# A row-fetched third tree, Silu in place in PSUM and a new order of work in a one-core layer of binding attention and tree feed-forward

## The chip, the cores and the metric

The kernel runs on one core of one Trainium2 chip. The metric is the device time of one execution, in microseconds. TensorE (PE) multiplies matrices, VectorE (DVE), ScalarE (ACT) and GpSimd (POOL) do the rest, and SyncE (SP) issues DMAs.

## The reference

Input x has 2 x 4096 tokens of D = 512. The layer is attention by binding, then a feed-forward made of trees, each on a layer norm and with a residual:

```python
q = unit(ln(x) @ Wq.T + bq); k = unit(...); v = unit(...)   # unit: FFT / (|FFT| + 1e-8)
s = cumsum(ifft(fft(k) * fft(v)).real, axis=tokens)
x = x + ifft(fft(s) * conj(fft(q))).real
logits = ln(x) @ W_in.T + b_in        # 8 trees of 255 nodes, 127 of them inner
# from the root, seven times: go right where the node's logit is positive
# dmap is 1 on the eight nodes of the path, in each tree
x = x + (silu(logits) * dmap) @ W_out.T
```

## The kernel before

Tokens go in 32 blocks of T = 256 (J = 2 halves of 128). The Fourier transform is folded into the projection weights in the prologue, so a projection gives the spectrum. Every product of TensorE is made of three fp16 products (high x high, high x low, low x high), so each operand is split in a high part by ScalarE (`high`, `act_high`, `fold_high`) and a low part by VectorE (`low`, `act_low`, `fold_low`). Weights stay in SBUF.

One queue per engine is written out by hand, and each engine runs its queue in order; semaphores join them. Each engine's program is `first()` (the prologue), `step(0)`, a loop over steps 1 to 29, and steps 30 and 31 written out. In `step(i)` the feed-forward of block i runs beside the attention of block n = i + 1:

- TensorE: `project(n, Q)`, K, V (48 matmuls each: a real part into `bank_p[0]`, then an imaginary one into `bank_p[1]`), `logits(i, t, c)` of tree t and its column slice c into `bank_l[t % 4]`, `counts(i, t)`, which adds the count of steps off the path, `down(i, j)` back to D, and the inverse transforms of block n (`transform_back`). Dense trees have two slices of 128 columns.
- Trees in `GATHERED` (0 and 1) have one dense slice, their inner nodes. For their last node on the path ScalarE's `leaf` marks it, one-column products give its number (`leaf_rows_of`, `leaf_row_copy`), POOL fetches its row of weights by an indirect DMA (`fetch`), VectorE multiplies (`leaf_dots`), ScalarE applies Silu (`leaf_silu`), and VectorE adds it (`leaf_add`).
- ScalarE: `evac_re` and `evac_im` of each projection, `square`, `root`, `high`, Silu of each tree into one of `HELD` = 3 buffers `acts` in SBUF, `act_high`. `logits` of tree t + 4 reuses a bank once Silu has read it.
- POOL: sums of squares, `add_eps`, `q_unit`, `bind` (four products k x v), the fetches, `unbind` (four products s x q, one after another) and its sums.
- VectorE: `residual`, statistics, low halves, reciprocals, `decide` (the comparison that feeds `counts`), `act_low`, the running sum, the small Nyquist operations (one frequency that is kept apart), leaf work and `result`.
- SP: the transposes of xn2 into `x2t` (for the logits) and of xn1 into `xt` (for the next projections), two DMAs each, and all loads and stores.

The prologue loads the projection weights, folds them (`fold_tile`), finds a scale for each of five groups of weights (Q, K, V, G_IN, G_OUT; ScalarE's `..._rows` sum absolute values, VectorE's `peak_of`, `peak_row` and `scale_group` follow), splits them, and does block 0's attention.

## Time and profile before

| | |
|---|---|
| median of 3 runs | 1975.06 us (1973.09 to 1975.19) |
| span of the profiled execution | 1972.4 us |
| outside its span | not listed; the median is 2.7 us above the span, the fastest run 0.7 us |
| TensorE busy | 1883.7 us, 96% of the span |
| VectorE busy | 1579.8 us, 80% |
| ScalarE busy | 1118.8 us, 57% |
| POOL busy | 917.0 us, 46% |

The page gives one execution of the program. Busy times of matmuls include their pipelined ends, so a busy TensorE isn't one at its peak. The prologue and step 0 last to 154.7 us, steps 1 to 30 to 1913.5.

### The profile page before, as it was taken

Reading aid. Unit: us, or ns where it says so; the run is one execution under the profiler, and the core shown is the slowest. Engines: PE = TensorE matmul, PEld = TensorE weight load, DVE = VectorE, ACT = ScalarE, POOL = GpSimd, SP = SyncE. Lnnn points to the kernel's source line nnn. Section 1 sums busy time; section 2 is a strip of 40 time slices with the busy share of each in tenths; the row PEclk is TensorE's granted clock in tenths of the full one; section 3 lists DMA queues with packets and bytes.
Section 4 is the critical chain, followed back from the end, with each engine's and each line's share of the span. In section 5 each row is a group of like instructions: output and inputs, shape, how many; then the busy total and the mean of one; then the engine's idle time right before and its main releaser. Section 6 shows DMA issues by size and latency. Waiting matters only on the chain.

```text
span 1972.4 us, 40210 instructions
## 1 busy us (share of the span) xinstructions
PE 1883.7 (96%) x14680; PEld 1410.5 (72%) x14680; DVE 1579.8 (80%) x2874; ACT 1118.8 (57%) x2151; POOL 917.0 (46%) x736
## 2 busy tenths in 40 slices
PE   8599999999999999999999999999999999999978
PEld 6468777777777777877777877777777777786755
DVE  4887888887888888788888788888788888878783
ACT  5566555566555556555556655556655555655543
POOL 1254444555444555444555444455544455534450
PEclk9799999999999999999999999999999999999998
DMA  8032133222223222223222213222222322222212
GB/s 278 11 86 87 54 96 95 65 85 85 64 85 96 75 80 80 82 67 96 83 77 85 85 53 96 94 66 85 85 64 85 96 75 79 81 71 79 86 54 65
DMA packets 181784, 163.18 MB, mean 83 GB/s; under 512 B 140160, under 2 KB 140800, under 8 KB 181760
## 3 DMA queue, kind: packets, MB, share of 16 engines
q1 hardware_dynamic: 163328, 95.48, 16.2%
q0 software_dynamic: 18432, 67.38, 10.2%
q8 instruction: 15, 0.25, 0.0%
q14 instruction: 9, 0.07, 0.0%
HBM read 95.72 MB, written 16.78 MB: 57 GB/s over the span
## 4 chain that ended last, share of the span: by engine, by line
PE 74%; DVE 10%; ACT 6%; issue 3%; DMA 0%; ACTq 0%; SPq 0%; DVEq 0%
PE bank_l L531 26%; PE bank_p L481 24%; PE bank_l L591 17%; DVE arena L1220 9%; ACT arena L796 3%; ACT arena L705 2%; PE bank_i L481 2%; PE bank_l L541 2%; ACT arena L806 1%; PE bank_i L552 1%; PE bank_i L562 0%; PE bank_i L559 0%; PE bank_i L560 0%; PE bank_i L561 0%; DVE sp_z L1178 0%
## 5 line engine op out<-in xcount | busy, mean ns | idle before, releaser
L591 PE MATMUL bank_l<-wout_mem,arena 128*128 128x512 f16 x2688 | 606.7, 379 | 38.6 <-DVE arena L1220 38.6
L531 PE MATMUL bank_l<-arena,win_mem 128*128 128x256 f16 x5376 | 626.0, 273 | 14.0 <-DMA arena<-xn_pair 14.0
L531 PEld LDWEIGHTS bank_l<-arena,win_mem 128*128 128x128 f16 x5376 | 527.5, 99 | 75.7 <-DMA arena<-xn_pair 14.2
L591 PEld LDWEIGHTS bank_l<-wout_mem,arena 128*128 128x128 f16 x2688 | 255.5, 98 | 365.8 <-DVE arena L1220 84.3
L481 PE MATMUL bank_p<-arena,wf_hi 128*128 128x256 f16 x3072 | 505.9, 273 | 2.7 <-ACT arena L742 2.7
L986 POOL TENSOR_TENSOR arena<-arena 128x512 f32<-128x512 f32 x96 | 121.9, 1270 | 658.5 <-ACT arena L751 658.5
L481 PE MATMUL bank_p<-arena,wf_lo 128*128 128x256 f16 x1536 | 419.1, 273 | 0.0
L1220 DVE SCALAR_TENSOR_TENSOR arena<-arena,s_act 128x512 f16<-128x512 f32 (+1 forms) x256 | 341.5, 1344 | 28.9 <-ACT arena L806 25.6
L481 PEld LDWEIGHTS bank_p<-arena,wf_hi 128*128 128x128 f16 x3072 | 299.7, 98 | 37.6 <-ACT arena L742 3.0
L796 ACT ACTIVATE arena<-bank_l,bias_in,s_logit 128x256 f32<-128x256 f32 x448 | 229.6, 556 | 142.0 <-PE bank_l L541 141.6
L1213 DVE TENSOR_SCALAR dec<-bank_l,thr,off 128x256 bf16<-128x256 f32 x256 | 135.8, 541 | 121.2 <-PE bank_l L531 120.0
L1063 POOL DMA_INDIRECT arena<-in_leaf_rows,leaf_row x128 | 138.6, 1083 | 113.1 <-issue 69.5
L806 ACT ACTIVATE arena<-arena,s_act 128x512 f16<-128x512 f32 (+1 forms) x256 | 166.7, 664 | 3.2
L481 PEld LDWEIGHTS bank_p<-arena,wf_lo 128*128 128x128 f16 x1536 | 150.5, 98 | 17.6
L1133 DVE RECIPROCAL arena<-arena 128x256 f32<-128x256 f32 x64 | 111.9, 1748 | 61.9 <-POOL arena L991 61.9
L908 ACT ACTIVATE odd<-bank_i 128x256 f32<-128x256 f32 x64 | 24.6, 384 | 170.7 <-PE bank_i L481 170.7
L1123 DVE TENSOR_TENSOR xn_pair<-arena,xn_pair 128x512 f16<-128x512 f32 x128 | 107.8, 864 | 9.5 <-ACT xn_pair L723 9.5
L784 ACT ACTIVATE leaf_act<-leaf_dot,arena 128x1 f32<-128x1 f32 x128 | 30.7, 287 | 144.2 <-DVE arena L1233 144.2
L1233 DVE SCALAR_TENSOR_TENSOR arena<-arena 128x512 f32<-128x512 f32 x128 | 111.2, 921 | 0.8 <-DMA arena<-in_leaf_rows,leaf_row 0.8
L1145 DVE RECIPROCAL arena<-arena 128x256 f32<-128x256 f32 x64 | 107.7, 1725 | 1.1
L991 POOL TENSOR_SCALAR arena<-arena,eps_s 128x512 f32<-128x512 f32 x64 | 45.6, 712 | 132.9 <-ACT arena L755 130.0
L728 ACT ACTIVATE arena<-bank_p,bias_f 128x256 f32<-128x256 f32 x192 | 80.7, 471 | 42.2 <-PE bank_p L481 42.2
(178 smaller groups left out, 2607.2 us busy)
## 6 DMA issues: line engine op xcount, KB each, us to landing
arena<-in_x SPq DMA_DIRECT2D x32, 512.0 KB, 3.4
arena<-arena SPq DMA_DIRECT2D x32, 512.0 KB, 2.9
out<-arena SPq DMA_DIRECT2D x64, 256.0 KB, 2.1
wout_mem<-in_w_in_t SPq DMA_DIRECT2D x1, 3584.0 KB, 14.6
arena<-in_w_out_t SPq DMA_DIRECT2D x1, 3584.0 KB, 14.6
arena<-xn_pair SPq DMA_TRANSPOSE x128, 2.7
arena<-in_leaf_rows,leaf_row POOLq DMA_INDIRECT x128, 5.6
win_mem<-in_wq SPq DMA_DIRECT2D x1, 1024.0 KB, 8.5
```

Of the source, the lines that this page charges most:

```text
L481: mm = pe.matmul(bank, a, b, start=(n == 0), stop=(n == len(pairs) - 1))
L531: mm = pe.matmul(bank_l[t % 4][:, c * T:(c + 1) * T], a[:, k, w:w + P], x2t[:, :, b, k, :], start=(c == 0 and k == 0 and m == 0), stop=((t ...
L591: mm = pe.matmul(bank_l[j][:, :], a[:, m, tok], w[:, m, :], start=(m == 0 and a is a_hi and w is wout_hi), stop=(m == DENSE - 1 and a is a ...
L796: ins = act.activation(acts[:, t % HELD, c * T:(c + 1) * T], bank_l[t % 4][:, c * T:(c + 1) * T], ACT.Silu, bias=bias_in[:, c, t:t + 1], s ...
L806: act.activation(a_hi[:, m:m + wide, :], acts[:, t % HELD, 0:wide * T].rearrange("p (c t) -> p c t", c=wide), ACT.Copy, scale=s_act[:, 0:1 ...
L986: pool.tensor_tensor(mag[:, q].rearrange("p c t -> p (c t)"), sq[:, 0:2].rearrange("p c t -> p (c t)"), sq[:, 2:4].rearrange("p c t -> p ( ...
L1063: pool.indirect_dma_start(fetched[:, g, j, :], None, leaf_rows, bass.IndirectOffsetOnAxis(leaf_row[:, g, j:j + 1], 0)).then_inc(leaf_fetch ...
L1123: dve.tensor_tensor(xn_pair[:, j, 1, :], xn[:, j, :], xn_pair[:, j, 0, :], ALU.subtract).then_inc(done, 1)
L1133: dve.reciprocal(mag[:, Q, h], mag[:, Q, h]).then_inc(rinv_ready, 1)
L1213: dve.tensor_scalar(dec[:, t % HELD, :], bank_l[t % 4][:, 0:T], thr[:, t:t + 1], off[:, 0:1], ALU.is_gt, ALU.mult).then_inc(dec_ready, 1)
L1220: dve.scalar_tensor_tensor(out=a_lo[:, m, :], in0=acts[:, t % HELD, 0:wide * T].rearrange("p (c t) -> p c t", c=wide), scalar=s_act[:, 0:1 ...
L1233: ins = dve.scalar_tensor_tensor(out=row, in0=row, scalar=1.0, in1=xn2[:, j, :], op0=ALU.mult, op1=ALU.mult, accum_out=leaf_dot[:, g, j:j ...
```

## The change

- `GATHERED` becomes (0, 1, 2): tree 2 keeps one dense slice, and its last node is fetched by row. There are 13 dense slices instead of 14.
- Silu writes back into its PSUM bank. `act_high` and `act_low` read there, `acts` goes, and `logits` and `down` wait for `act_low` before they reuse a bank. `HELD`, now 4, is left for `dec` alone.
- The Nyquist sums take two products of three columns instead of five of one.
- The projections are numbered and run K, V, Q. The orders of all engines within a step follow, in the prologue too: weights arrive and fold as K, V, Q, TensorE begins with `WARM` = 30 products of ones, and block 1's projections come ahead of block 0's inverse transforms (`first_back`).
- POOL waits after each product of the unbinding.

The diff, cut to its core:

```diff
-GATHERED = (0, 1)
+GATHERED = (0, 1, 2)
-HELD = 3
+HELD = 4
-Q, K, V, G_IN, G_OUT = range(5)
+K, V, Q, G_IN, G_OUT = range(5)
@@ logits
-                    pe.wait_ge(act_ready, TREES * i + t - 3)
+                    pe.wait_ge(a_lo_ready, TREES * i + t - 3)
@@ nyquist_sums
-                pe.matmul(sp_sums[:, 0:1], upper, sp_kv[:, 0:1], start=True, stop=True)
-                pe.matmul(sp_sums[:, 1:2], upper, sp_kv[:, 1:2], start=True, stop=False)
-                pe.matmul(sp_sums[:, 1:2], full, sp_kv[:, 0:1], start=False, stop=True)
-                pe.matmul(sp_sums[:, 2:3], full, sp_kv[:, 0:1], start=True, stop=False)
-                pe.matmul(sp_sums[:, 2:3], full, sp_kv[:, 1:2], start=False, stop=True).then_inc(sp_sums_full, 1)
+                pe.matmul(sp_sums[:, 0:3], upper, sp_kv[:, 0:3], start=True, stop=False)
+                pe.matmul(sp_sums[:, 0:3], full, sp_kv[:, 2:5], start=False, stop=True).then_inc(sp_sums_full, 1)
@@ down
-                pe.wait_ge(act_ready, TREES * i + 5 + j)
+                pe.wait_ge(a_lo_ready, TREES * i + 5 + j)
@@ TensorE, first()
+                warm_up()
+                pe.wait_ge(dft_in, 16 * 2)
+                fold_tile(K, 0)
+                bound_of(K)
+                fold_tile(K, 1)
+                fold_tile(K, 2)
+                bound_of(V)
                 bias_fold()
+                fold_tile(K, 3)
+                for m in range(KT):
+                    fold_tile(V, m)
+                bound_of(Q)
+                pe.wait_ge(xt_ready, 16 * J)
+                project(0, K)
                 fold_tile(Q, 0)
...
+                project(0, V)
+                pe.wait_ge(win_in, 16 * 3)
+                for m in range(1, KT):
+                    fold_tile(Q, m)
+                peaks_in_row(G_IN)
                 project(0, Q)
...
@@ TensorE, step
-                    project(n, Q)
                     project(n, K)
                     project(n, V)
+                    project(n, Q)
+                if isinstance(i, int) and i == 0:
+                    first_back()
                 logits(i, 0, 0)
                 logits(i, 1, 0)
                 counts(i, 0)
                 logits(i, 2, 0)
-                logits(i, 2, 1)
+                counts(i, 1)
...
@@ ScalarE, silu
-                if t >= HELD:
-                    act.wait_ge(a_lo_ready, TREES * i + t + 1 - HELD)
-                elif not isinstance(i, int) or i:
-                    act.wait_ge(a_lo_ready, TREES * i)
                 for c in [c for c in range(2) if (t, c) in COLUMN]:
-                    ins = act.activation(acts[:, t % HELD, c * T:(c + 1) * T], bank_l[t % 4][:, c * T:(c + 1) * T],
+                    ins = act.activation(bank_l[t % 4][:, c * T:(c + 1) * T], bank_l[t % 4][:, c * T:(c + 1) * T],
@@ ScalarE, first(): behind the evacuation of Q of block 0
+                high(1, xn1, ln1_done, xn1_hi_ready)
+                root(0, Q)
+                win_high(0)
+                win_high(1)
+                win_high(2)
+                win_high(3)
                 for c in range(PIECES):
                     wout_rows(c)
+                act.wait_ge(bound, 1)
+                for q in (K, V):
+                    evac_re(1, q)
+                    evac_im(1, q)
@@ ScalarE, step
+                if attn and not begun:
                     evac_re(n, K)
+                    evac_im(n, K)
+                if attn:
+                    square(n, K)
+                if attn and not begun:
+                    evac_re(n, V)
                 std(i, mv2, rs2, ln2_mv, ln2_std)
+                if attn:
+                    root(n, K)
+                if attn and not begun:
+                    evac_im(n, V)
...
                 high(i, xn2, ln2_done, xn2_hi_ready)
...
+                if attn:
+                    square(n, V)
+                if attn and not begun:
+                    evac_re(n, Q)
+                if attn:
+                    root(n, V)
+                if attn and not begun:
+                    evac_im(n, Q)
+                if attn:
+                    square(n, Q)
@@ POOL, unbind
+                pool.tensor_tensor(prod[:, 0], sr, qr, ALU.mult).then_inc(z_prod, 1)
+                pool.wait_ge(z_prod, 4 * n + 1)
+                pool.tensor_tensor(prod[:, 1], si, qi, ALU.mult).then_inc(z_prod, 1)
...
@@ POOL, step
+                    sum_squares(n, K)
+                    add_eps(n, K)
+                    sum_squares(n, V)
                     sum_squares(n, Q)
                     add_eps(n, Q)
-                    sum_squares(n, K)
-                    sum_squares(n, V)
-                    add_eps(n, K)
+                    bind(n)
                     q_unit(n)
-                    bind(n)
-                fetch(i, 1)
-                fetch(i, 0)
+                for g in range(LEAVES):
+                    fetch(i, g)
@@ VectorE, nyquist_bind
-                dve.tensor_tensor(sp_kv[:, :], sp_hat[:, :, K], sp_hat[:, :, V], ALU.mult).then_inc(sp_kv_ready, 1)
+                dve.tensor_tensor(sp_kv[:, 0:2], sp_hat[:, :, K], sp_hat[:, :, V], ALU.mult)
+                dve.tensor_tensor(sp_kv[:, 3:4], sp_hat[:, 0, K:K + 1], sp_hat[:, 0, V:V + 1], ALU.mult).then_inc(sp_bound, 1)
+                dve.wait_ge(sp_bound, n + 1)
+                dve.tensor_tensor(sp_kv[:, 4:5], sp_kv[:, 0:1], sp_kv[:, 1:2], ALU.add).then_inc(sp_kv_ready, 1)
```

VectorE's queue in `step`, from `low(i)` on, is now `next_stats`, `kv_denominator`, `kv_inverse(0)`, `decide(0)`, `kv_inverse(1)`, `decide(1)`, (in step 0 `wout_low(2)` and `(3)`), `k_scale`, `decide(2)`, `act_low(0)`, `q_inverse(0)`, `act_low(1)`, `decide(3)`, `q_inverse(1)`, `act_low(2)`, three Nyquist operations, `decide(4)`, `scale_and_shift`, `nyquist_bind`, `act_low(3)`, `running_sum`, `decide(5)`, and so on to `act_low(7)`, the low halves of xn1, three `leaf_dots`, `carries`, three `leaf_add` and `result`. In `first()` its `running_sum(0)` comes before `peak_of(G_IN)`, and `nyquist_unbind(0)` before `win_low(1)` to `(3)`, `peak_of(G_OUT)` and `scale_group(G_OUT)`. In step 0 ScalarE does four `wout_high` behind `high(0)` instead of two.

## Rows read from the trace of the kernel before

**Rows 1.** The page: busy time by engine, and TensorE's granted clock in 40 slices.

```profile
PE 1883.7 (96%) x14680; PEld 1410.5 (72%) x14680; DVE 1579.8 (80%) x2874; ACT 1118.8 (57%) x2151; POOL 917.0 (46%) x736
...
PEclk9799999999999999999999999999999999999998
```

**Rows 2.** The chain that ended last: start us, us, what.

```profile
154.87 15.72 PE bank_p L481 x144
...
1021.52 10.53 PE bank_l L591 x48
...
1032.05 1.36 PE bank_i L481 x24
...
1051.97 5.24 PE bank_l L531 x48
...
1855.11 15.72 PE bank_p L481 x144
```

**Rows 3.** Timeline of TensorE: start us, us, instruction, [idle before, releaser].

```profile
1033.25 0.38 PE L481 MATMUL bank_p<-arena,wf_hi 128*128 128x256 f16 x2
...
1066.11 0.28 PE L558 MATMUL bank_i<-sp_kv,running 128*128 128x1 f32 x2
...
1067.14 0.60 PE L541 MATMUL bank_l<-dec,path 128*128 128x256 bf16 x4
...
1076.73 1.47 PE L591 MATMUL bank_l<-wout_mem,arena 128*128 128x512 f16 x6 [0.76 <-DVE arena L1220]
...
1927.71 4.66 PE L531 MATMUL bank_l<-arena,win_mem 128*128 128x256 f16 x21 [14.05 <-DMA arena<-xn_pair]
```

**Rows 4.** Timeline of ScalarE in the same block.

```profile
1038.69 0.47 ACT L738 ACTIVATE sp_raw<-bank_p,bias_f 1x256 f32<-1x256 f32 x1 [1.78 <-PE bank_p L481]
...
1043.20 1.15 ACT L723 ACTIVATE xn_pair<-arena 128x512 f16<-128x512 f32 x2 [0.87 <-DVE arena L1104]
...
1050.65 1.06 ACT L751 ACTIVATE arena<-arena 128x1024 f32<-128x1024 f32 x1
...
1053.74 1.28 ACT L796 ACT_TABLE_LOAD   x1
```

**Rows 5.** SP's timeline in that block, and the page's DMA issues (us to landing).

```profile
1044.64 2.58 SPq L340 DMA_TRANSPOSE arena<-xn_pair  x2
...
arena<-xn_pair SPq DMA_TRANSPOSE x128, 2.7
```

**Rows 6.** Timeline of VectorE in that block.

```profile
1054.77 3.37 DVE L1145 RECIPROCAL arena<-arena 128x256 f32<-128x256 f32 x2
...
1060.68 0.15 DVE L1158 TENSOR_TENSOR sp_den<-bank_i,eps_sp 128x6 f32<-128x6 f32 x1
...
1064.12 0.55 DVE L1117 SCALAR_TENSOR_TENSOR nb<-mv,rs 128x2 f32<-128x2 f32 x1
...
1067.04 1.38 DVE L1193 TENSOR_TENSOR_SCAN arena<-arena,carry 128x256 f32<-128x256 f32 x2
...
1069.62 0.72 DVE L1220 SCALAR_TENSOR_TENSOR arena<-arena,s_act 128x512 f16<-128x512 f32 x1
...
1072.44 5.91 DVE L1220 SCALAR_TENSOR_TENSOR arena<-arena,s_act 128x512 f16<-128x512 f32 x2
```

**Rows 7.** Timeline of POOL in that block.

```profile
1059.54 1.44 POOL L1009 TENSOR_TENSOR arena<-arena 128x512 f32<-128x512 f32 x1 [2.45 <-DVE arena L1151]
...
1063.39 1.27 POOL L1012 TENSOR_TENSOR arena<-arena 128x512 f32<-128x512 f32 x1
...
1065.94 1.01 POOL L1063 DMA_INDIRECT arena<-in_leaf_rows,leaf_row  x1 [1.28 <-issue]
...
1071.18 1.27 POOL L1019 TENSOR_TENSOR arena<-arena 128x512 f32<-128x512 f32 x1
```

**Rows 8.** Groups by line and shape: busy us, mean ns, idle before.

```profile
L813 ACT ACTIVATE win_mem<-wout_mem,sc 128x1792 f16<-128x1792 f32 x4 | 7.1, 1776 | 0.0
...
L840 ACT ACTIVATE arena<-arena 128x1792 f32<-128x1792 f32 x4 | 6.8, 1693 | 0.3
```

More of the change, by code:

```diff
@@ L864, in first @@
                     fold_high(m)
-                for c in range(PIECES):
-                    win_rows(c)
-                    fold_high(KT + c)
+                projection_rows(Q)
+                for m in range(KT):
+                    fold_high(KT + m)
                 act.wait_ge(consts_done, 1)
+                evac_re(0, K)
+                evac_im(0, K)
+                square(0, K)
+                fold_high(2 * KT)
+                root(0, K)
+                win_rows(0)
+                win_rows(1)
+                evac_re(0, V)
+                evac_im(0, V)
+                square(0, V)
+                fold_high(2 * KT + 1)
+                root(0, V)
+                fold_high(2 * KT + 2)
+                win_rows(2)
+                fold_high(2 * KT + 3)
+                win_rows(3)
+                std(1, mv1, rs1, ln1_mv, ln1_std)
                 evac_re(0, Q)
@@ L897, in first @@
                 act.activation(z_hi[:, 2:4, :], prod[:, 2], ACT.Copy).then_inc(z_hi_ready, 1)
-                wout_high(0)
-                wout_high(1)
+                evac_re(1, Q)
+                evac_im(1, Q)
             def step(i, attn, nxt):
@@ L963, in step @@
                 silu(i, 7)
+                act_high(i, 7)
                 if nxt:
@@ L1487, in step @@
                 if isinstance(i, int) and i == 0:
+                    wout_low(0)
+                    wout_low(1)
+                if nxt:
+                    next_stats(n + 1)
+                if attn:
+                    kv_denominator(n)
+                    kv_inverse(n, 0)
+                decide(i, 0)
+                if attn:
+                    kv_inverse(n, 1)
+                decide(i, 1)
+                if isinstance(i, int) and i == 0:
                     wout_low(2)
```

266 lines of the change are left out of this document (113 added, 153 removed).

## The prediction

> **What bounds the kernel now.** Read first the page's busy line [rows 1]: TensorE is busy 96% of the span, so a gain must come from fewer or better packed matmuls. Then the chain that ended last [rows 2]: a block of 256 tokens starts with 144 projection matmuls, and from the one at 154.87 us (block step 1) to the one at 1855.11 (step 30) lie 29 blocks, 58.63 us each. The same rows give TensorE's pitches: 15.72/144 = 0.109 us for 256 columns, 10.53/48 = 0.219 for 512, 1.36 for both inverse transforms. A block's matmuls fill 57.4 us. The rest is 1.17 us of waiting in `down`: 0.76 for VectorE's `act_low` [rows 3], then twice 0.2. The third view is the timeline of one block on each engine [rows 3 to 7]; I write its times from the block's first projection matmul, 1033.25 us, as t. The span has three parts: 154.7 us to t = 0 of step 1, 30 blocks (1758.8), and 58.9 from 1913.5 to the end.
>
> **TensorE's own work.** A third tree fetched by row takes one 128-column slice out of the logits (12 matmuls, 1.31 us) and six 512-column matmuls out of `down` (1.32). The Nyquist sums go from ten records between 1066.11 and 1067.14 [rows 3] to four, about 0.6 us less. Two more one-column products cost 0.05. So TensorE's floor falls from 57.4 to 54.25 us. The question is whether the other engines allow it in the new order, so I walk a block through.
>
> **First wait: x2t.** The projections now run K, V, Q. ScalarE before took `high(i)` at t = 9.95 (1043.20 [rows 4]) and only then the second evacuation of the middle projection. Now `root(K)` and `evac_im(V)` stand before `high(i)`. `evac_im` of the first projection started at t = 5.44, 0.2 behind its 48 matmuls [rows 4]; that of V's must follow 96 matmuls, at 10.48 + 0.2 = 10.68. Its three instructions take 1.30, so `high(i)` moves to t = 11.98, 2.03 us later. Behind it: the low halves, then two transposes on SP. The first was issued 1.44 after `high`; SP needs 1.34 until the second, which lands 2.7 after its issue [rows 5]: 11.98 + 1.44 + 1.34 + 2.7 = 17.46. Before, the same sum gave 15.43, 0.29 ahead of the first logit at 15.72. The wait is now 1.85 us with its release, at every block.
>
> **Second wait: VectorE before `decide(5)`.** V's chain is next: square at 13.16 (1.06), POOL's sum (1.27), root at 15.6 (0.63), so `kv_denominator` starts at 16.3. Then 0.8 for it, 1.7 for a reciprocal (two in 3.37 [rows 6]), a short wait for the logits of tree 0 (19.1), `decide` 0.46, 1.7, 0.46, `k_scale` 1.2, 0.46: t = 23.4. Now a wait for ScalarE, which has Q's evacuation, square and root ahead of the leaf, the table load (1.28) [rows 4], Silu and `act_high`: 24.07. Before, Q came first in the block and was off this path. On from there: `act_low`, reciprocal, `act_low`, `decide`, reciprocal, `act_low`, three small Nyquist operations (0.58) and `decide` are 6.2: t = 30.3.
> Here `scale_and_shift` meets POOL. It has two SBUF inputs of two elements, and took 0.55 us because it started at 1064.12, inside POOL's last product of `bind`, which ended at 1064.66 [rows 6, 7]. In the new order `bind` runs from 23.04 for 5.12 us and `q_unit` follows from 28.8 (the second reciprocal of Q) with two products back to back until 31.28. So 1 us goes to waiting. Then 0.35 for `nyquist_bind` with its added wait, 0.67 for `act_low(3)`, 2.58 for the scans (from 1067.04 to the next start at 1069.62 [rows 6]), 0.57 for `decide(5)`: t = 35.45.
> TensorE comes to `counts(5)` at t = 33.75: 17.57 + 13 slices less the last two (12 matmuls each; 132 in all, 14.4), five counts (1.1), the leaf and Nyquist rows (0.6) and 0.1 for `decide(1)`. It waits 1.7 us. What follows is counts (3 x 0.22), tree 7 (2.62), sums (0.45), 78 matmuls of `down` (17.1), 0.24 for changes of shape and 1.36: 22.4. The period is 57.9 us.
>
> **What lies beside.** Bank reuse now waits for `act_low` instead of Silu: logits 4 to 7 want it at 25.3, 28.3, 31.1 and 35.6, and it is done at 24.5, 26.6, 29.1 and 32.3, so this costs nothing, by a margin of 0.8 at the tightest. The 1.17 us in `down` goes: `act_low(7)` ends at 43.9, its matmuls start at 46.5. That rests on the PSUM source. Before, two `act_low` took 5.91 us [rows 6], being shut out by POOL's four products without a gap; a VectorE operation with one input in PSUM was not: the 0.15 us one at 1060.68 runs inside POOL's 1.44 us product of 1059.54 [rows 6, 7]. The Trainium skill's page SBUF — State Buffer, Who interferes with whom, says so in general: VectorE with two SBUF inputs contends with a GpSimd operation that reads SBUF, whoever starts first holds the port for the whole instruction, and one with at most one SBUF input does not contend. By that rule the move of Silu helps, and the same rule is what stops `scale_and_shift`; rows and rule agree. I take 0.67 to 0.75 us for 512 elements; shut out, it would be as in the second rival. POOL: six row fetches at 1.31 instead of four (the four began at 1065.94 and the products behind them at 1071.18 [rows 7]), so its unbinding starts at about 39.8; with the waits between its products VectorE gets in after each. z is ready by about 52, needed at 56.5. VectorE's end of block: two more dots and two more adds, 2.6 us, and five or six operations that each lose about 0.9 to POOL. It ends at 59.5, 1.6 behind the next block's start. Residual and statistics have 2.4 us of room before `root(K)` and `next_stats` feel it: hidden, with 0.8 to spare. Silu written to PSUM: the same 0.56, bounds 0.46 to 0.65, beside 8 us of free ScalarE.
>
> **The prologue** is where most is lost. Four orders matter.
> (a) `peak_of(G_IN)` now stands on VectorE behind `running_sum(0)`, and `project(0, Q)` behind `peaks_in_row(G_IN)` on TensorE. K's projection should start at about 33 (36.0 before: the warm-up saves folds at half rate, K's weights come first). V's root follows at 52; denominator, two reciprocals, three `fold_low`, `k_scale`, four products and the scans are 12.7: the peak is at 65, while TensorE has been done since 54.
> (b) Q's projection then runs in part at the lower clock level, 1.2 GHz (before, the granted clock was 0.7 in the slice from 49 to 99 us, where TensorE had waited [rows 1]; I take 20 of the 48 matmuls at half rate, 7.4 us for 5.24), to 73. `high(1)` is behind Q's evacuation: 75.8. Transposes land at 81.3, and `project(1, K)` runs 81.3 to 88.8.
> (c) ScalarE still has root (0.6), four `win_high` at 1.74 and four `wout_rows` at 1.83 (1.69 and the read of the sum, in part hidden) [rows 8] before `evac_re(1, K)`: 91.8. So V and Q of block 1 end at about 105.
> (d) `nyquist_sums(0)` is behind these, and `nyquist_unbind(0)` holds up three `win_low` (2.0 each) and G_OUT's peak: 113. The peak's two products, then the inverse transforms: 117.
> Before, those transforms ended at 91.7 and the first logit came at 111.3, 42.9 plus 0.5 before t = 0 of step 1 (the projection lay between). Now it needs residual, normalisation and transposes, 14.05 us after a transform (at 1927.71 [rows 3]), then a start at half rate, four `wout_high` (7) and two more `wout_low` (4) before the chain above: 64.3 us to the next block. Sum 181.5, 26.8 later. Bounds: 15 (the DMAs and folds 4 earlier, wait (c) half hidden) to 33.
> **Last step.** No attention, so none of the two waits: 58.9 less 2.6 = 56.3.
> **Sum.** 181.5 + 30 x 57.9 (1737.0) + 56.3 = 1974.8, against 154.7 + 1758.8 + 58.9 = 1972.4. The median shown is 1975.06, 2.7 above this span, so 1977.5 us, 0.1% more.
>
> **Rivals.** *1, much faster:* one or both waits are not there. Without the second the period is 17.57 + 38.6 = 56.2; without either 54.25. The sums are 1924 and 1865 span, with 2.7 about 1927 and 1868. For it: VectorE is idle about a fifth of a block, and my second wait is a sum of twenty small terms. Against it: both come out of order within one queue, not out of load. *2, slower:* an `act_low` out of PSUM is still shut out. `act_low(0)` at 24.07 falls in `bind`, which has no waits inside, and comes free at 28.16: the chain and the period grow by up to 4.1, to 62, span 2098. It decides from 0.05 us per block on (the 1.5 us between the forecast and 1979.0, over 30 blocks). Against it is the row of 1060.68. *3, slower:* the end of the block on VectorE. Each us beyond its 0.8 of room is one us of period; 1 us too much gives 57.9 + 1 and a time of 2008. The six contended operations are what speaks for it. *4, faster:* the prologue costs nothing: 1951.
>
> **How the numbers follow.** Forecast 0.55, with its own range 1962 to 1997 (period 57.5 to 58.5, prologue 20 to 30). Rival 1 0.22, rival 4 0.07, rival 3 0.12, rival 2 0.04. A no-change band of 0.2% is 1971.1 to 1979.0, about what a measurement can tell from none. Of the forecast's 0.55, 0.12 lies below, 0.15 within, 0.28 above. Faster 0.12 + 0.29 = 0.41; same 0.16; slower 0.28 + 0.15 = 0.43. The range leaves out the floor and the shut-out: 1924 to 2008.
>
> **What would show it.** TensorE waits for a DMA at each block's first logit, near 1.85 us, and for `dec` at `counts(5)`, near 1.7; none in `down`. `act_low` of 512 elements at 0.75 us in all. `scale_and_shift` about 1 us. First logit near 131 us, with TensorE idle near 54 to 65 and about 106 to 114. It is wrong if `high(i)` starts within 10.5 us of the first projection, if `decide(5)` is written before TensorE asks, or if t = 0 of step 1 comes before 165.

## The result: 1976.0 us, 0.2% slower, and the profile after

The changed kernel took 1976.0 us (median of 20 runs), the kernel before 1973.1 us (20 runs) beside it: ratio 1.0022, 95% interval 1.0013 to 1.0032. The forecast was 1977.5 us. Run again beside three experiments it took 1973.1 (12 runs), ratio 1.0013 (0.9998 to 1.0029). So the change costs between nothing and 0.3%. The profiled execution has a span of 1980.1 us.

The page of the kernel after: busy time, the granted clock, three groups of TensorE, two of VectorE (busy us, mean ns, idle before and its releaser), and the landing of the transposes.

```profile
PE 1801.5 (91%) x14036; PEld 1350.3 (68%) x14036; DVE 1598.6 (81%) x3130; ACT 1130.4 (57%) x2215; POOL 943.7 (48%) x801
...
PEclk8779999999999999999999999999999999999998
...
L535 PE MATMUL bank_l<-arena,win_mem 128*128 128x256 f16 x4992 | 601.3, 278 | 99.2 <-DMA arena<-xn_pair 99.2
...
L592 PE MATMUL bank_l<-wout_mem,arena 128*128 128x512 f16 x2496 | 549.1, 379 | 0.0
...
L1253 DVE SCALAR_TENSOR_TENSOR arena<-bank_l,s_act,arena 128x512 f16<-128x512 f32 (+1 forms) x256 | 160.1, 625 | 146.1 <-ACT arena L814 146.1
...
L1266 DVE SCALAR_TENSOR_TENSOR arena<-arena 128x512 f32<-128x512 f32 x192 | 216.0, 1182 | 0.0
...
L545 PE MATMUL bank_l<-dec,path 128*128 128x256 bf16 x512 | 98.0, 273 | 45.3 <-DVE dec L1246 45.3
...
arena<-xn_pair SPq DMA_TRANSPOSE x128, 3.1
```

Beside [rows 1]: TensorE's busy time fell by 82 us, 1883.7 to 1801.5, and the span did not follow. Two groups show where the time is: the logits (L535) waited 99.2 us for the transposes of x2t, 33 of them in step 0 and the last step, the counts (L545) 45.3 us for `dec`. `down` (L592) waited for nothing. `act_low` (L1253) takes 0.63 us on average over both of its widths, and 0.75 at 512 elements, where the 512-element rows in [rows 6] took up to 2.96.

Timelines of the kernel after in a block whose first projection starts at 1051.38 (t = 0). TensorE first:

```profile
1069.45 2.79 PE L535 MATMUL bank_l<-arena,win_mem 128*128 128x256 f16 x24 [2.19 <-DMA arena<-xn_pair]
...
1087.01 0.39 PE L545 MATMUL bank_l<-dec,path 128*128 128x256 bf16 x2 [1.37 <-DVE dec L1246]
...
1090.00 0.36 PE L563 MATMUL bank_i<-sp_kv,running 128*128 128x3 f32 x2
```

ScalarE, VectorE and POOL of the same block:

```profile
1063.00 0.46 ACT L754 ACTIVATE arena<-bank_p,bias_f 128x256 f32<-128x256 f32 x1
1063.36 1.14 ACT L735 ACTIVATE xn_pair<-arena 128x512 f16<-128x512 f32 x2
```

```profile
1081.81 1.12 DVE L1147 SCALAR_TENSOR_TENSOR nb<-mv,rs 128x2 f32<-128x2 f32 x1
...
1083.85 1.38 DVE L1226 TENSOR_TENSOR_SCAN arena<-arena,carry 128x256 f32<-128x256 f32 x2
...
1086.43 0.52 DVE L1246 TENSOR_SCALAR dec<-bank_l,thr,off 128x256 bf16<-128x256 f32 x1
...
1109.14 1.41 DVE L1314 SCALAR_TENSOR_TENSOR arena<-bank_l,s_out,arena 128x512 f32<-128x512 f32 x2
1110.96 0.28 DVE L1293 SCALAR_TENSOR_TENSOR arena<-bank_i,sp_z,odd 128x64 f32<-128x64 f32 x1 [0.41 <-DVE arena L1314]
```

```profile
1081.65 1.26 POOL L1025 TENSOR_TENSOR arena<-arena 128x512 f32<-128x512 f32 x1
```

`high` starts at t = 11.98, right behind the second evacuation of V, as forecast to the hundredth, and the two waits are those of the forecast: 2.19 us (forecast 1.85) and 1.37 us (1.7). VectorE ends the block (1109.14 + 1.41) 1.7 us behind the next block's first projection at 1108.85 (forecast 1.6), and its `residual` starts 0.4 later, 2.1 behind it.

From one start of the inverse transforms to the next are 57.2 to 57.5 us in 20 of the 30 blocks, 59.1 in nine, and 61.5 in one. The windows of 4 us behind the first logit show what the nine have (columns: length, busy time and instructions of PE, PEld, DVE, ACT, POOL, the granted clock, DMA):

```profile
1126.96:1130.96 4.00, 4.00 (x37) 3.59 (x38) 3.04 (x4) 2.29 (x5) 1.96 (x2) 1.00 0.00 0
1184.45:1188.45 4.00, 4.00 (x22) 2.96 (x23) 2.00 (x3) 1.40 (x3) 1.95 (x2) 0.57 0.00 0
```

Both blocks waited 2.2 us for x2t. In the second TensorE then ran for most of 4 us at its lower level, 1.2 GHz: 22 matmuls instead of 37, 1.67 us lost. That was in no term of the forecast.

The block of 61.5 has such a fall too, and longer waits: POOL was idle for 2.43 us ahead of its last row fetch instead of 0.30, VectorE's `residual` began 3.9 us behind the block's first projection instead of 2.1, and TensorE waited for V's evacuation and then 3.08 us for x2t. POOL, then TensorE:

```profile
1208.19 0.94 POOL L1093 DMA_INDIRECT arena<-in_leaf_rows,leaf_row  x1 [2.43 <-issue]
```

```profile
1240.08 0.39 PE L484 MATMUL bank_p<-arena,wf_hi 128*128 128x256 f16 x2 [1.29 <-ACT arena L754]
```

So VectorE's end of block, hidden in the others, shows once by itself. Why the fetch came late is not shown.

TensorE's waits in the prologue and step 0:

```profile
69.54 0.58 PE L475 MATMUL bank_l<-arena,mxp 128*1 128x128 f32 x2 [10.95 <-DVE mxp L1324]
...
87.18 0.61 PE L484 MATMUL bank_p<-arena,wf_hi 128*128 128x256 f16 x2 [6.97 <-DMA arena<-xn_pair]
...
115.08 0.59 PE L475 MATMUL bank_l<-arena,mxp 128*1 128x128 f32 x2 [7.48 <-DVE mxp L1324]
...
136.92 2.31 PE L535 MATMUL bank_l<-arena,win_mem 128*128 128x256 f16 x10 [17.59 <-DMA arena<-xn_pair]
```

They stand where orders (a), (b) and (d) of the forecast put them. Step 1 begins at 181.2 us (forecast 181.5, before 154.7); the last step takes 56.2 (56.3).

### The profile page after: what moved, and what is told of

The parts are those of the page before. It is cut to its first block and busy times, and to the rows that moved or that the text cites. A ratio compares the mean times of both kernels' runs of the same rounds, so it can differ in the third digit from the quotient of the medians.

```text
span 1980.1 us, 39683 instructions
## 1 busy us (share of the span) xinstructions
PE 1801.5 (91%) x14036; PEld 1350.3 (68%) x14036; DVE 1598.6 (81%) x3130; ACT 1130.4 (57%) x2215; POOL 943.7 (48%) x801
## 5 line engine op out<-in xcount | busy, mean ns | idle before, releaser
L535 PE MATMUL bank_l<-arena,win_mem 128*128 128x256 f16 x4992 | 601.3, 278 | 99.2 <-DMA arena<-xn_pair 99.2
L535 PEld LDWEIGHTS bank_l<-arena,win_mem 128*128 128x128 f16 x4992 | 493.5, 100 | 172.2 <-issue 72.0
L592 PE MATMUL bank_l<-wout_mem,arena 128*128 128x512 f16 x2496 | 549.1, 379 | 0.0
L592 PEld LDWEIGHTS bank_l<-wout_mem,arena 128*128 128x128 f16 x2496 | 244.1, 98 | 281.0
L804 ACT ACTIVATE bank_l<-bank_l,bias_in,s_logit 128x256 f32<-128x256 f32 x416 | 210.6, 534 | 201.9 <-PE bank_l L545 198.3
L1253 DVE SCALAR_TENSOR_TENSOR arena<-bank_l,s_act,arena 128x512 f16<-128x512 f32 (+1 forms) x256 | 160.1, 625 | 146.1 <-ACT arena L814 146.1
L1093 POOL DMA_INDIRECT arena<-in_leaf_rows,leaf_row x192 | 184.3, 960 | 90.2 <-issue 53.2
L1266 DVE SCALAR_TENSOR_TENSOR arena<-arena 128x512 f32<-128x512 f32 x192 | 216.0, 1182 | 0.0
L814 ACT ACTIVATE arena<-bank_l,s_act 128x512 f16<-128x512 f32 (+1 forms) x256 | 155.5, 607 | 5.3
L1276 DVE SCALAR_TENSOR_TENSOR arena<-arena,leaf_act 128x512 f32<-128x512 f32 x192 | 135.3, 745 | 6.6
L545 PE MATMUL bank_l<-dec,path 128*128 128x256 bf16 x512 | 98.0, 273 | 45.3 <-DVE dec L1246 45.3
```

The source lines that it names most:

```text
L535: mm = pe.matmul(bank_l[t % 4][:, c * T:(c + 1) * T], a[:, k, w:w + P], x2t[:, :, b, k, :], start=(c == 0 and k == 0 and m == 0), stop=((t ...
L592: mm = pe.matmul(bank_l[j][:, :], a[:, m, tok], w[:, m, :], start=(m == 0 and a is a_hi and w is wout_hi), stop=(m == DENSE - 1 and a is a ...
L804: ins = act.activation(bank_l[t % 4][:, c * T:(c + 1) * T], bank_l[t % 4][:, c * T:(c + 1) * T], ACT.Silu, bias=bias_in[:, c, t:t + 1], sc ...
L814: act.activation(a_hi[:, m:m + wide, :], bank_l[t % 4][:, 0:wide * T].rearrange("p (c t) -> p c t", c=wide), ACT.Copy, scale=s_act[:, 0:1] ...
L1093: pool.indirect_dma_start(fetched[:, g, j, :], None, leaf_rows, bass.IndirectOffsetOnAxis(leaf_row[:, g, j:j + 1], 0)).then_inc(leaf_fetch ...
L1253: dve.scalar_tensor_tensor(out=a_lo[:, m, :], in0=bank_l[t % 4][:, 0:wide * T].rearrange("p (c t) -> p c t", c=wide), scalar=s_act[:, 0:1] ...
```

## The experiments

Each was compared with the kernel before on the same chip in the same stretch; four chips served, one after the other (e1 to e4; c0, e5, e8, e10; e9, e11, e12; e14). "Base period" is that of most blocks at full clock.

| kernel | median us (runs) | ratio to before, 95% | base period, us |
|---|---|---|---|
| changed kernel | 1976.0 (20) | 1.0022 (1.0013 to 1.0032) | 57.45 |
| e1_high_first | 1976.2 (8) | 1.0015 (1.0004 to 1.0027) | 57.8 |
| e2_decide5_early | 1979.4 (7) | 1.0038 (1.0027 to 1.0050) | 57.75 |
| e3_shift_early | 1980.1 (7) | 1.0040 (1.0028 to 1.0051) | 57.7 |
| e4_busy_wait | 1969.2 (10) | 0.9990 (0.9977 to 1.0003) | 57.75 |
| c0_after | 1973.1 (12) | 1.0013 (0.9998 to 1.0029) | 57.43 |
| e5_dec5_dec7 | 2026.5 (5) | 1.0274 (1.0255 to 1.0292) | 58.3 |
| e8_prologue | 1964.7 (5) | 0.9957 (0.9945 to 0.9970) | 57.45 |
| e10_silu_sbuf | 2085.5 (5) | 1.0564 (1.0543 to 1.0585) | 58.4 to 64.2, all blocks |
| e9_prol_busy | **1946.1** (4) | **0.9874** (0.9859 to 0.9889) | 57.44 |
| e11_no_gaps | 1982.2 (12) | 1.0034 (1.0020 to 1.0048) | 57.45 |
| e12_light_end | 1945.4 (4) | 0.9859 (0.9845 to 0.9873) | 55.9 |
| e14_early_dots | 1953.8 (4) | 0.9890 (0.9873 to 0.9906) | 57.5 |

### The first wait: high ahead of V's evacuation

```diff
                 if attn:
                     root(n, K)
-                if attn and not begun:
-                    evac_im(n, V)
                 if attn:
                     act.wait_ge(xt_ready, 16 * J * (n + 1))
                 high(i, xn2, ln2_done, xn2_hi_ready)
+                if attn and not begun:
+                    evac_im(n, V)
```

> ScalarE takes high(i) ahead of the second half of V's evacuation. My theory: both waits of TensorE are set by order within a queue, and the later one is counted from the block's start, not from the first logit. high then ends about 1.05 us earlier (the normalised x is there at 1062.9, high ends at 1064.5 in the block of 1051.38), so the wait for x2t falls from 2.2 to about 1.15 us, of which 0.4 turns up as a wait of Q's imaginary part for its bank. But V's square, root and so VectorE's chain to decide(5) end 0.4 later, so the wait at counts(5) grows from 1.4 to between 2.4 and 2.9, and the period stays at 57.4 to 57.9 us. If the fall of the granted clock in every third block hangs on the long wait for x2t, it becomes rarer: 17 us less, 1963 us by this run's own before; else 1976 to 1990. Rival (the transposes, not their start, set the wait: DMA bound): the wait for x2t stays at 2.2.

TensorE in one block of this kernel:

```profile
1115.18 0.39 PE L484 MATMUL bank_p<-arena,wf_hi 128*128 128x256 f16 x2 [0.36 <-ACT arena L754]
...
1118.83 2.79 PE L535 MATMUL bank_l<-arena,win_mem 128*128 128x256 f16 x24 [0.85 <-DMA arena<-xn_pair]
...
1137.27 0.58 PE L545 MATMUL bank_l<-dec,path 128*128 128x256 bf16 x2 [1.94 <-DVE dec L1246]
```

2.2 + 1.4 us of waiting became 0.36 + 0.85 + 1.94. So the first wait is the order on ScalarE, and taking it away pays nothing, because the second is counted from the block's start: `counts(5)` comes at t = 35.7 in this block and at 35.6 in the kernel after. Time unchanged, as expected.

The low clock moved along with the waiting. Five blocks took 59.2 and five 58.4, and in each of these the clock fell behind the wait of 1.9 to 2.1 us at `counts(5)`, not behind x2t:

```profile
1137.30:1141.30 4.00, 4.00 (x22) 2.96 (x23) 1.77 (x3) 1.68 (x3) 3.37 (x4) 0.57 0.88 298
```

### The second wait: decide(5) ahead of the scans

```diff
+                decide(i, 5)
                 if attn:
                     running_sum(n)
-                decide(i, 5)
                 act_low(i, 4)
```

> VectorE does decide(5) before the four scans instead of behind them. My theory (the wait at counts(5) is order, not load): dec is there 2.6 us earlier, the 1.37 us of waiting at counts(5) goes, nothing takes its place, and the period falls from 57.45 to 56.1 us: 30 blocks x 1.37 = 41 us less, about 1935 us. Rival (VectorE is the bound, as in the forecast's third rival): the work pushed behind comes late at the block's end or at the next decide, a wait of 1 us or more turns up there, and the time stays within 0.5% of 1976.

The wait at `counts(5)` went, and one of 1.69 us came at `counts(7)`. TensorE's sum and VectorE in this kernel:

```profile
1083.56 0.36 PE L563 MATMUL bank_i<-sp_kv,running 128*128 128x3 f32 x2
```

```profile
1087.03 0.22 DVE L1211 SCALAR_TENSOR_TENSOR sp_z<-bank_i,sp_carry,sp_hat 128x2 f32<-128x2 f32 x1 [3.20 <-remote]
1087.20 0.55 DVE L1246 TENSOR_SCALAR dec<-bank_l,thr,off 128x256 bf16<-128x256 f32 x1
```

`decide(7)` stands behind `nyquist_unbind` (L1211), and that started 3.47 us behind TensorE's sum that releases it (1083.56), instead of 0.40 in the kernel after (1090.00, 1090.40). ScalarE's Silu of tree 6 waited 4.2 us with it. None of the 41 us came. What came is what the rival said, a wait at the next `decide` and a time within 0.5%, but not for its reason: VectorE was idle for 3.20 us there. Neither the theory nor the rival named this signal.

### scale_and_shift away from q_unit

```diff
+                if nxt:
+                    scale_and_shift(n + 1)
                 if attn:
                     k_scale(n)
...
                 decide(i, 4)
-                if nxt:
-                    scale_and_shift(n + 1)
```

> scale_and_shift is taken ahead of k_scale on VectorE, so that it no longer falls into the two products of q_unit on POOL. My theory: its second operation took 1.12 us there and takes 0.2 to 0.55 here (POOL runs its product of bind or nothing beside it), decide(5) comes about 0.95 us earlier, the wait at counts(5) falls from 1.37 to about 0.4 and the period by as much: 28 us less, about 1948 us. Rival (the time of that operation is not what decides when decide(5) comes, since what follows waits for something else): decide(5) at the same place in the block, time unchanged within 0.2%.

VectorE of this kernel, then POOL:

```profile
1068.56 0.16 DVE L1147 SCALAR_TENSOR_TENSOR nb<-mv,rs 128x2 f32<-128x2 f32 x1
...
1076.60 1.25 DVE L1204 TENSOR_TENSOR sp_kv<-sp_hat 128x1 f32<-128x1 f32 x1
```

```profile
1076.58 1.26 POOL L1025 TENSOR_TENSOR arena<-arena 128x512 f32<-128x512 f32 x1
```

The moved operation fell from 1.12 to 0.16 us, and the next one with two SBUF inputs, one element wide, took 1.25 instead of 0.15. Each ends with POOL's second product (1082.91 in the kernel after, 1077.84 here). What costs is that product, which follows the first without a gap; which small operation meets it is all the same. The wait at `counts(5)` fell from 1.37 to 1.25 only. The rival was right: what follows waited for something else, the same product of POOL. That the scans would have waited for it as well is not shown.

### TensorE kept busy while x2t comes

```diff
+                if attn and not (isinstance(i, int) and i == 0):
+                    for _ in range(16):
+                        pe.matmul(bank_l[3][:, 0:T], wf_hi[:, 0, 0, 0:P], wf_hi[:, 0, 1, 0:T], start=True, stop=True)
                 logits(i, 0, 0)
```

> Adds 16 products of 256 columns into a free bank ahead of a block's first logit in steps 1 to 30, about 1.75 us of work that nobody uses, so that TensorE is busy while x2t comes. The output's arithmetic is unchanged. My theory: the wait of 2.2 us shrinks to 0.4 to 0.5 with the products in its place, so blocks with full clock stay at 57.4 us; and the fall of the granted clock in every third block (1.67 us each, 10 blocks) no longer happens: 17 us less, about 1960 us. Rival (the clock falls for the work itself, not behind the idle stretch): the falls stay or become more, and the time is unchanged or longer.

Windows of 4 us behind the first logit of two blocks in a row:

```profile
1116.96:1120.96 4.00, 4.00 (x37) 3.58 (x38) 3.26 (x4) 2.38 (x5) 1.96 (x2) 1.00 0.00 0
1174.72:1178.72 4.00, 4.00 (x37) 3.59 (x38) 3.10 (x4) 2.37 (x5) 1.96 (x2) 1.00 0.00 0
```

The granted clock never fell in the loop, where the control below has eight falls, and over the whole execution it is 0.982 against 0.977. Two long blocks are left at full clock: the first (59.1, x2t late) and one of 60.2. So the low clock in the loop comes from TensorE idling, as e1_high_first said from the other side. The time is 9 us above the 1960 expected. The base period was 57.75, 0.3 longer, as in all four kernels of this stretch, and 30 times that is the 9 us: VectorE again began `nyquist_unbind` 1.9 us behind the sum, and `decide(7)` with it.

### The changed kernel again, and both decides early

> The changed kernel again, unchanged. In its first profile nyquist_unbind on VectorE and Silu of tree 6 on ScalarE started 0.4 us behind the sums on TensorE that release them; in the four experiments so far, run together, they started 1.1 to 3 us behind. If that is the run or the chip, it is to be seen here too, with periods of 57.75 us where the first profile had 57.45, and a time of 1978 to 1984 us. If it comes from the edits, it is not, and the time is 1976.

Base period 57.43, `nyquist_unbind` 0.4 us behind the sum, 1973.1 us. So the late signal belonged to the chip or the runs of the first four, not to the changed kernel. The loop has eight falls of the clock, 13.7 us in all; the first profile had ten, 17.1 us. The median also hides two groups: nine runs from 1970.1 to 1975.8 and three from 1981.6 to 1984.1. In the table's first row six of 20 runs are in the upper group, at 1981.4 to 1983.5, and the profiled one is of them. Here is the difference, the window from 21 to 34 us, first in the profile after, then in this one:

```profile
21.00:34.00 13.00, 13.00 (x31) 8.97 (x30) 4.19 (x13) 3.78 (x5) 0.00 (x0) 0.50 1.07 301
```

```profile
21.00:34.00 13.00, 13.00 (x71) 10.16 (x70) 6.06 (x25) 5.21 (x7) 0.00 (x0) 1.00 1.05 307
```

In some executions TensorE folds weights there at 1.2 GHz with no idle time ahead of it, in others at 2.4. The first inverse transforms start at 116.56 in the one and 109.02 in the other: 7.5 us. The kernel before has no such second group: its 84 runs beside all these lie from 1970.6 to 1976.1. So the split came with the changed kernel.

```diff
+                decide(i, 5)
                 if attn:
                     running_sum(n)
-                decide(i, 5)
...
+                decide(i, 7)
                 if attn:
                     nyquist_unbind(n)
-                decide(i, 7)
```

> decide(5) ahead of the scans, and decide(7) ahead of nyquist_unbind on VectorE. In the experiment with decide(5) alone the wait of 1.37 us at counts(5) went and one of 1.69 came at counts(7), because decide(7) stands behind nyquist_unbind, which started 3 us behind the sums of TensorE. My theory (order alone): with decide(7) free of it, no wait for dec is left, the period falls to 56.1 us, and the time by 30 x 1.4 to 1.7 = 40 to 50 us, to about 1935. Rival (VectorE or ScalarE is loaded): another wait of more than 1 us turns up in down for act_low(5) to act_low(7), or at the next block's first projections, and less than half of it is gained.

The signals came in time here and no wait for `dec` was left in the loop. Still it was 2.7% slower. TensorE of this kernel, then VectorE at the start of the same block (first projection at 1068.41):

```profile
1082.96 0.39 PE L484 MATMUL bank_p<-arena,wf_hi 128*128 128x256 f16 x2 [1.28 <-ACT arena L754]
...
1088.82 1.37 PE L535 MATMUL bank_l<-arena,win_mem 128*128 128x256 f16 x11 [3.07 <-DMA arena<-xn_pair]
```

```profile
1070.43 1.41 DVE L1314 SCALAR_TENSOR_TENSOR arena<-bank_l,s_out,arena 128x512 f32<-128x512 f32 x2
1072.25 0.28 DVE L1293 SCALAR_TENSOR_TENSOR arena<-bank_i,sp_z,odd 128x64 f32<-128x64 f32 x1 [0.41 <-DVE arena L1314]
```

`residual` is now 3.84 us behind the first projection (2.1 before), the statistics with it; ScalarE's square root for them stands ahead of `root(K)` and V's evacuation, so Q's projection waits 1.28 us for its bank, and x2t comes 0.9 later still. 1.28 + 0.9 - 1.37 = +0.8: the base period 58.3. Most blocks now also have the low clock and take 59.5 to 60.0 (26 falls in the loop, 46 us). In the changed kernel the wait of 1.37 us at `counts(5)` was the room that VectorE's end of block lived on. These are the two waits that the block of 61.5 us in the kernel after had by accident.

### VectorE's end of block made shorter

```diff
                 for j in range(J):
-                    row = fetched[:, g, j, 0:D]
+                    w = 2 if g == 2 else D
+                    row = fetched[:, g, j, 0:w]
```

and the same width in `leaf_add`, on top of e5_dec5_dec7. It leaves the third fetched leaf out.

> The experiment with decide(5) and decide(7) early, which took 2026 us with periods of 59.5 to 60.0 us, and in it the dots and adds of the third fetched tree over 2 columns instead of 512, so that its leaf is not computed: VectorE's end of block is 2.4 to 3.5 us shorter. My theory: that end sets the period there (result, residual, statistics, x2t, logits, and back), so TensorE's wait of 1.28 us for evac_im goes, that for x2t falls from 3.1 to about 2.2, and the period to 56.2 to 57 us: 1920 to 1945 us. Rival (POOL's late unbinding, or the two decides, set it): the waits stay and the period remains above 58.5.

TensorE's groups of this kernel:

```profile
L535 PE MATMUL bank_l<-arena,win_mem 128*128 128x256 f16 x4992 | 620.6, 283 | 97.5 <-DMA arena<-xn_pair 97.5
...
L545 PE MATMUL bank_l<-dec,path 128*128 128x256 bf16 x512 | 99.1, 276 | 2.4 <-DVE dec L1246 2.4
```

Waiting for `dec` is gone (45.3 to 2.4 us), the wait for V's evacuation too, x2t is back at 2.2 us, and the base period is 55.9. So VectorE's end is what the two early decides ran into: the dots and adds of one tree separate 2026 from 1945 us. In 22 of the 30 blocks the clock fell once more, and 21 of them take 57.5 to 57.7: 37 us in all. The profiled execution began at half clock and took 1950.9 us; the other three took 1944.9 to 1945.5.

### Silu's output back in SBUF

```diff
-                    ins = act.activation(bank_l[t % 4][:, c * T:(c + 1) * T], bank_l[t % 4][:, c * T:(c + 1) * T],
+                    ins = act.activation(acts[:, t % AH, c * T:(c + 1) * T], bank_l[t % 4][:, c * T:(c + 1) * T],
```

with `AH` = 3 buffers, `act_high` and `act_low` reading them, and their waits as before.

> The changed kernel with Silu's output back in SBUF (three buffers, as before); everything else of the change stays. My theory: act_low has two SBUF inputs again and is shut out by POOL's products: its mean goes from 0.63 us to 1.0 or more, the ones in the unbinding to over 1.2 each (fewer than before, as POOL now waits between products), those of trees 0 to 2 under bind and q_unit up to 2.5 us, so decide(5) comes 1 to 4 us later: the period rises to between 58.5 and 61.5 us, the time to between 2008 and 2095. Rival (the source makes no difference, POOL's gaps let VectorE in): act_low 0.7 to 0.8 us, time within 0.3% of the changed kernel.

VectorE and POOL in one block, and the wait at `counts(5)` on TensorE:

```profile
1060.69 1.52 DVE L1259 SCALAR_TENSOR_TENSOR arena<-arena,s_act 128x256 f16<-128x256 f32 x1 [1.02 <-ACT arena L820]
```

```profile
1060.66 1.27 POOL L1042 TENSOR_TENSOR arena<-arena 128x512 f32<-128x512 f32 x1
```

```profile
1073.73 0.39 PE L547 MATMUL bank_l<-dec,path 128*128 128x256 bf16 x2 [2.33 <-DVE dec L1252]
```

256 elements took 1.52 us inside POOL's `bind`, where the kernel after takes 0.42 on average. The wait at `counts(5)` is 2.33 us and the periods are 58.4 to 64.2: 112 us above the control. Silu in PSUM alone is worth that much in this order; in the loop ScalarE's Silu waits for TensorE alone, so the three buffers cost nothing. Some 43 of the 112 us are the low clock, though, 33 falls in the loop against eight. The Trainium skill's page SBUF — State Buffer, Who interferes with whom, has it so: a VectorE operation with at most one SBUF input, outside its two-port modes, does not contend with POOL. The trace agrees, 0.42 against 1.52 us.

### The waits between POOL's products taken out

```diff
-                pool.tensor_tensor(prod[:, 0], sr, qr, ALU.mult).then_inc(z_prod, 1)
-                pool.wait_ge(z_prod, 4 * n + 1)
+                pool.tensor_tensor(prod[:, 0], sr, qr, ALU.mult)
```

and the same for the next two.

> Takes the waits between POOL's four products of the unbinding out again, as before the change; nothing else. My theory: the products take 5.0 us instead of 5.3, and VectorE, which has low_of and the dots there, is shut out through all that remain instead of one at a time; work with a PSUM input (act_low, decide) isn't. low_of and the first dots come 0 to 1.5 us later, VectorE's end of block by as much; since the block's cycle runs through that end (result, residual, x2t), the period grows by 0 to 1.5 us, time +0 to +45 us. Rival: POOL finishes 0.3 us earlier and frees VectorE as much earlier, so period and time fall by up to 0.3 us a block, 9 us.

The base period is 57.45, as with the waits. The median of 1982.2 comes from the start: seven of twelve runs lie at 1981.5 to 1984.1 and five at 1972.3 to 1975.3, the two groups of the control. VectorE's `residual` came 1.78 us behind the block's start instead of 2.11, the 0.3 us that the rival named, but the period did not follow. These waits neither cost nor gain time; my theory gave at least nothing, and nothing it was.

### Another order in the prologue

TensorE projects Q ahead of G_IN's peak, and G_OUT's peak stands behind the inverse transforms. The main moves:

```diff
@@ TensorE
-                peaks_in_row(G_IN)
                 project(0, Q)
+                peaks_in_row(G_IN)
@@ ScalarE
-                for c in range(PIECES):
-                    wout_rows(c)
                 act.wait_ge(bound, 1)
                 for q in (K, V):
                     evac_re(1, q)
                     evac_im(1, q)
+                    wout_rows(2 * q)
+                    wout_rows(2 * q + 1)
@@ VectorE
-                nyquist_unbind(0)
-                nyquist_carry(0)
-                first_z_low()
                 win_low(1)
                 win_low(2)
                 win_low(3)
+                nyquist_unbind(0)
+                nyquist_carry(0)
+                first_z_low()
```

> Undoes three of the four orders of the prologue that the forecast charged: TensorE projects Q of block 0 ahead of G_IN's peak, VectorE takes that peak, the normalisation of block 1 and the last low halves of Q's weights ahead of the scans; ScalarE evacuates K and V of block 1 ahead of wout_rows; win_low 1 to 3 stand ahead of nyquist_unbind(0), and G_OUT's peak behind the inverse transforms. My theory: TensorE's waits of 10.95, 6.97, 1.46 and 7.48 us ahead of the first transforms shrink to 8 us or less in all, the first inverse transforms start at 98 to 104 us instead of 116.6, the first logit by as much earlier, and the whole is 12 to 18 us shorter. Rival (a chain elsewhere, the loads or the folds, sets it): the transforms stay within 5 us of 116.6 and the gain is under 5 us.

TensorE of this kernel:

```profile
71.50 0.61 PE L484 MATMUL bank_p<-arena,wf_hi 128*128 128x256 f16 x2 [10.65 <-DMA arena<-xn_pair]
...
92.09 0.22 PE L484 MATMUL bank_i<-tab_hi,arena 128*128 128x129 f16 x1 [1.87 <-DVE arena L1427]
...
115.72 1.67 PE L535 MATMUL bank_l<-arena,win_mem 128*128 128x256 f16 x7 [20.15 <-DMA arena<-xn_pair]
```

The transforms start at 92.1 instead of 109.0 (control, same full clock at the start), more than expected, though the waits ahead of them still sum to 16 us (28.7 in the control), not 8; step 1 begins 13.8 us earlier, at 159.9, and not 17, because G_OUT's peak and scale now stand ahead of `residual`, which starts 5.2 us behind the transforms instead of 2.1. The whole is 8.4 us shorter than the control, where 12 to 18 were expected: the loop had eleven falls of the clock against eight, which take 5.1 back.

### The two gains together, and a last try

> The prologue of the earlier experiment and, as in another, 16 products of 256 columns ahead of the first logit of steps 1 to 30. My theory: the gains add, since one ends before the loop and the other is the granted clock in it: no block of 59.1 us is left, 10 x 1.67 = 17 us less than the prologue alone (1964.7), so 1948 us. Rival (the longer periods of 57.75 us of the first four experiments come with an added product, not with that run): 30 x 0.3 = 9 us of it are lost, 1957 us.

1946.1 us, 1.3% faster than the kernel before; all periods are 57.3 to 57.5 but two (58.9 at the start, 59.4), and the clock never fell in the loop. It computes the whole layer.

```diff
+                leaf_dots(i, 0)
                 act_low(i, 7)
```

on top of it and of the two early decides, with dots 1 and 2 left where they were.

> The kernel with the other prologue and the 16 added products (1946.1 us, periods of 57.44), and in it decide(5) ahead of the scans, decide(7) ahead of nyquist_unbind, and the two dots of the first fetched tree ahead of act_low(7), where VectorE waited 1.2 us for ScalarE. Nothing is left out of the computation. My theory: the wait for dec goes, as in the two experiments with those decides; what they lost was VectorE's end of block, which was 1.7 us later than in the changed kernel (residual 3.84 us behind the first projection instead of 2.1), and the dots in the wait take about 1.2 us off it. So the wait for evac_im stays under 0.5 us, and the period comes to 56.3 to 57.2 us: 1946 less 30 x 0.25 to 1.1, 1912 to 1938 us. Rival (the dots there only meet POOL's products, 1.6 us each instead of 0.7, so that act_low(7) and the end come as late as before): periods of 58 us or more, 1963 us and above.

VectorE and TensorE of this kernel:

```profile
1013.25 0.54 DVE L1249 TENSOR_SCALAR dec<-bank_l,thr,off 128x256 bf16<-128x256 f32 x1 [3.13 <-remote]
```

```profile
1013.86 0.39 PE L545 MATMUL bank_l<-dec,path 128*128 128x256 bf16 x2 [1.45 <-DVE dec L1249]
```

TensorE's late signal was back, on the fourth chip, and now `decide(7)` itself waited for it. So this doesn't tell whether the dots in the gap help: `residual` came 2.17 us behind the first projection, not 3.84, but TensorE's wait of 1.45 us gave VectorE as much room. Neither the period of the theory (56.3 to 57.2) nor the rival's (58 or more) came, and the question stays open.

## Why the prediction was right, point by point

- **TensorE's floor.** Forecast 54.25 us. Measured 57.45 - 2.2 - 1.37 = 53.9. The difference lies behind `counts(5)`: 22.4 us were said to the block's end, 21.8 are measured.
- **First wait.** Forecast 1.85, measured 2.2. `high` came when it was said; the transposes landed after 3.1 us instead of 2.7 [rows 5]. Undone in e1_high_first: the wait went where the order said.
- **Second wait.** Forecast 1.7, measured 1.37. `counts(5)` came at t = 35.6 (forecast 35.45), and TensorE was ready for it 0.5 us later than said, 0.35 of it by the longer first wait: in the main the errors of the two waits are one and cost the period nothing. `scale_and_shift` took 1.12 us, where about 1 was said. That moving it would give its time back was not said, and is not so (e3_shift_early).
- **The period.** Forecast 57.9. The base is 57.45: the floor and the second wait were 0.7 too large together, the first wait 0.35 too small. Ten falls of the clock at 1.7 us, one of them in the block of 61.5, make the mean 58.1 in the profiled run. The forecast allowed for the low clock in the prologue alone, so this term, 0.6 a block, was left out; the kernel before had no fall in its loop, although it waited 2.5 us once.
- **Silu in PSUM.** Forecast free and the cure of the waits in `down`: both so. Rival 2, dead with a chance of 0.04, has its price from e10_silu_sbuf: up to 4.1 us a block was said, and 3.5 on average was measured with the source in SBUF ((2073.5 - 1968.6) / 30), of which 1.4 is the low clock.
- **VectorE's end.** The forecast gave it 0.8 us of room, in rival 3. V's evacuation has 0.34 (ScalarE's idle time ahead of it), and e5_dec5_dec7 used it up. This rival was no mishap that might befall the kernel; it is the bound behind the second wait. The block of 61.5 us is its one appearance in the kernel after.
- **Rival 1.** "Without the second wait the period is 56.2" was wrong as it stood. Without it the period was 58.3, and 55.9 only with a tree's dots and adds gone as well.
- **The prologue.** Step 1 was to begin at 181.5; it began at 181.2 in the profiled run, but 7.5 us of that are the half clock from 21 to 34 us, which no term had. Without it (control) it is 173.7. So the sum was 8 too large (its parts, 117 and 64.3, add up to 181.3): the peak came 2.5 earlier than said, xt of block 1 1.7, the transforms' end (110.4) 6.6, and step 0 took 63.3 instead of 64.3. e8_prologue gave 13.8 of the 19 us back by the orders that the forecast named.
- **Outside the span.** Forecast 2.7 us, taken from a median of three runs. Measured 1.9 (1981.96 against 1980.1), and the kernel before has a median of 1973.1 in 20 runs. So the time of 1977.5 was said to be 0.1% above the kernel before, and 1976.0 is 0.15% above it by its median; both are near nothing.

In sum, for the control's profile against [rows 2]: 30 x (57.96 - 58.63) = -20 us in the loop, -2.7 in the last step, +19 in the prologue, so -3.8 (1968.6 against 1972.4). At full clock the loop gained 1.1 us a block (57.45 against 58.57), 34 us, and the falls of the clock take 14 of them back; the executions that start at half clock add 7.5. The reasons held in the main, and the nearness of 1977.5 to 1976.0 owes something to errors that cancelled: a base period 0.45 too long against the clock, a prologue 8 too long against the half clock.

## What to carry to other kernels

A wait in one queue can be the room that another engine lives on: before a wait is taken out, walk the cycle (here result, residual, statistics, transposes, logits) and ask what is late next. An operand moved from SBUF to PSUM was worth more here than any of the orders tried, where POOL runs long products beside VectorE. Where TensorE must idle a couple of microseconds ahead of a long stretch, products that nobody uses can be cheaper than the clock that it loses.

## What the runs showed of the hardware

- **The clock behind a short wait.** A wait of 2.2 us ahead of the logits was followed by 0.57 of granted clock over 4 us in every third block, and by 1.00 in the others; with 16 products in its place it never was (e4_busy_wait, e9_prol_busy). In e12_light_end it was 22 blocks of 30, and in e1_high_first, where the longest wait is the one of 2 us at `counts(5)`, the clock fell behind that one. In the kernel before a single wait of 2.54 us brought no fall. What picks the block is not shown.
- **Half clock without idling.** From 21 to 34 us TensorE ran at 0.50 in some executions and at 1.00 in others, with the same busy time ahead of it; it costs 7.5 us and splits the runs in two groups. The kernel before has one group alone; what starts it is not shown.
- **POOL's products without a gap hold off VectorE's smallest work.** An operation of one element with two SBUF inputs took 1.25 us instead of 0.15 (e3_shift_early).
- **Late signals from TensorE.** In five profiles, those of two chips, VectorE and ScalarE began 1.8 to 3.9 us behind the sum or count on TensorE that releases them, in most blocks and 1.1 to 1.6 us after POOL's last row fetch. In the profiles of the two other chips, and in the first one after, `nyquist_unbind` began 0.4 us behind it (0.6 where `decide(7)` stands ahead). e4_busy_wait and e9_prol_busy, alike in the loop, lie on either side: 57.75 and 57.44 us. The kernel before took 1973 us on all four. That it hangs on the chip is argued from this, not shown.
